# A four-part graph network on one core: its six edge passes rewritten, with sums of parts in PSUM, bf16 scatter, stored one-hots, four gather tiles and a lag of two turns

## What is computed

```
for l in range(3):                                   # message net
    m = concatenate([x[src], x[dst], ew], -1)
    m = relu(m @ edge_W[l] + edge_b[l])
    agg = segment_sum(m, dst, n)
    x = relu(concatenate([x, agg], -1) @ node_W[l] + node_b[l])
...
h0 = relu(x @ W_enc + b_enc)                         # relation net
agg = segment_sum(einsum('nd,rdo->rno', h0, W_rel)[edge_type, src], dst, n)
...
for Wl, b, Wr in ((W1l, b1, W1r), (W2l, b2, W2r)):   # sage net
    h = relu(segment_sum(h[src], dst, n) / deg @ Wl + b + h @ Wr)
```

## Time and profile before

| | |
|---|---|
| median of three runs | 13509.89 us |
| lowest, highest | 13503.28, 13514.92 us |
| span of the profiled execution | 13453.0 us |
| PE, DVE, ACT, POOL busy | 83%, 81%, 39%, 18% |
| TensorE clock granted, mean | 0.949 |
| message passes (first gather to last scatter) | 848, 784, 783 us |
| relation pass | 1220 us |
| sage passes | 566, 566 us |
| from there to the end (attention) | 6314 us |

### The profile page before, as it was taken

How to read it: one execution, slowest core, us unless ns; L and a number is a source line. 1 busy time by engine, 2 the same in 40 slices (tenths; PEclk the granted TensorE clock), 3 DMA queues, 4 the chain that set the end, 5 groups by cost and what they waited for, 6 DMA issues and landing times. The chain is left out here.

```text
span 13453.0 us, 456368 instructions
## 1 busy us (share of the span) xinstructions
PE 11137.4 (83%) x106911; PEld 9882.7 (73%) x106912; DVE 10911.2 (81%) x40164; ACT 5227.5 (39%) x19100; POOL 2409.1 (18%) x7659
## 2 busy tenths in 40 slices
PE   3555399899899599976665879999998789999998
PEld 3444388799798499975553339999997338999998
DVE  6545399688688288876565999999997999999998
ACT  1000022122222022235452338865453337875454
POOL 2777300000000000001110001112221001222222
PEclk9999999899899599999896999999998999999999
DMA  1111177444243011113231554432221554432222
GB/s 54 47 50 47 45 228 236 138 128 128 80 128 115 4 41 41 41 50 88 71 87 51 148 140 115 115 92 73 70 73 47 143 147 113 115 98 73 70 73 61
DMA packets 1206840, 1232.94 MB, mean 92 GB/s; under 512 B 218352, under 2 KB 1042801, under 8 KB 1206107
## 3 DMA queue, kind: packets, MB, share of 16 engines
q1 hardware_dynamic: 1180954, 1228.47, 32.8%
q0 software_dynamic: 25792, 3.35, 0.2%
HBM read 1115.06 MB, written 116.16 MB: 92 GB/s over the span
## 5 line engine op out<-in xcount | busy, mean ns | idle before, releaser
L993 DVE TENSOR_SCALAR hot<-iota_row,place 128x128 f32<-128x128 f16 (+1 forms) x9000 | 1818.8, 269 | 158.5 <-PE acc L1092 135.7
L1711 ACT ACTIVATE msgs<-G,share 128x64 f32<-128x64 f32 x6000 | 1395.6, 315 | 1346.0 <-PE G L1725 1346.0
L985 DVE TENSOR_SCALAR hotT<-idx,iota_col 128x512 bf16<-128x512 f16 x4500 | 1323.8, 352 | 524.4 <-PE G L1138 492.1
L1725 PE MATMUL G<-u_b,hotT 128*128 x12000 | 1592.2, 276 | 50.3 <-DVE hotT L1659 50.3
L1735 PE MATMUL S<-msgs,hot 128*128 128x128 f32 x12000 | 1586.3, 275 | 0.0
L1157 ACT CAST msgs<-G 128x384 bf16<-128x384 f32 x2250 | 1020.4, 480 | 1372.7 <-PE G L1138 1368.1
L1725 PEld LDWEIGHTS G<-u_b,hotT 128*128 128x128 f32 x12000 | 1467.4, 193 | 51.0 <-issue 51.0
L1735 PEld LDWEIGHTS S<-msgs,hot 128*128 128x128 f32 x12000 | 1462.3, 192 | 0.0
L1080 PE MATMUL G<-table_m,hotT 128*128 x9000 | 1309.8, 248 | 93.4 <-issue 69.3
L1110 ACT ACTIVATE msgs<-sums 128x128 f32<-128x128 f32 x2250 | 699.3, 311 | 1762.3 <-DVE sums L1102 1400.5
L1547 ACT ACTIVATE msgs<-G,msgs 128x64 f32<-128x64 f32 x6000 | 1315.5, 333 | 30.5 <-issue 21.0
(11 more groups left out here) (323 smaller groups left out, 19877.9 us busy)
## 6 DMA issues: line engine op xcount, KB each, us to landing
idx<-pos_rows SPq DMA_DIRECT2D x6375, 128.0 KB, 2.9
hotT<-hots_d SPq DMA_DIRECT2D x750, 256.0 KB
hots_d<-hotT SPq DMA_DIRECT2D x375, 256.0 KB, 3.4
key_b<-key_rows SPq DMA_DIRECT2D x62, 416.0 KB
ty_b<-type_rows SPq DMA_DIRECT2D x62, 416.0 KB
rows<-rel_rows SPq DMA_DIRECT2D x1500, 6.0 KB
ew_now<-ew_rows_d SPq DMA_DIRECT2D x1125, 3.0 KB
sorted_d<-recs,place POOLq DMA_INDIRECT x806
```

Source lines behind the costliest of these rows:

```text
L985: op = eng.tensor_scalar(hotT[:, c % deep, n], idx[:, c, r], p.col[:, first:first + 1], None, ALU.is_equal)
L993: op = eng.tensor_scalar(hot[:, c % 2, q], p.row16[:], place[:, c % 2, q:q + 1], None, ALU.is_equal)
L1711: op = eng.activation(msgs[:, c % 2, 2 + j // HEADS, j % HEADS * D:(j % HEADS + 1) * D], G[c % 2][1][:, j * D:(j + 1) * D], ACT.Copy, scal ...
L1725: mm = eng.matmul(G[c % 2][b][:, k * W:(k + 1) * W], hotT[:, c % 2, q * P:(q + 1) * P], table[:, ds(dst_at(at, q, 24 * W), W)], start=True ...
```

## The change

It touches the six passes alone.

- The table's three parts lie one behind the other (`[P, 3, BLK * D]`). In message passes each part is a product of its own of 64 columns, and all seven products of a chunk (three source, three destination, one with nine rows of edge weights) add up in the same 64 columns of `G`, so the reduction on DVE goes. ACT applies the relu from PSUM to an f32 tile `whole`.
- The message is split into three bf16 values for the scatter: the upper halves of `whole`'s words, the upper halves of `left` = whole - upper half, and `low` = left - its upper half, the last two made by DVE. Three bf16 products of 64 columns a chunk replace the f32 one. In the first pass a product of two columns a chunk counts the degrees.
- The first message pass stores its scatter one-hots and source one-hots together; all later passes load the scatter one-hots, the later message passes the source ones too, and these build the destination ones from `idx`. POOL's copies stay in the first pass alone.
- The table `acc` has 64 columns a block (four banks in place of five), and there are four `G` tiles. PE scatters turn t-2 after the gather of turn t. DMAs fetch two turns at a time, and `hots`, `idx` are eight turns deep.
- In the sage passes DVE evicts one half of `G` and ACT the other; in the relation pass ACT does both. A gather product there stays one of 192 columns.

The core of the diff:

```diff
                 def gather(t, c, at):
+                    ready(eng, turned, t + 1)
+                    ready(eng, relud, t + 1)
+                    for q in range(4):
+                        to = G[c % 4][:, q * D:(q + 1) * D]
+                        for side in range(2):
+                            place_of = dst_at(at, q, LAST) if side else src_at(at, LAST)
+                            for part in range(3):
+                                eng.matmul(to, hots[:, c, 1 + side, q * P:(q + 1) * P], s.table3[side][:, part, ds(place_of, D)],
+                                           start=(side == 0 and part == 0), stop=False)
+                        mm = eng.matmul(to, s.ew_now[:, c, q * P:(q + 1) * P], s.we9[:, l], start=False, stop=True)
...
+                def scatter(t, c, was):
+                    ready(eng, made, t + LAG + 1)
+                    for q in range(4):
+                        hot = hots[:, c, 0, q * P:(q + 1) * P]
+                        at = dst_at(was, q, LAST)
+                        to = acc[:, ds(at, D)]
+                        if degrees:
+                            eng.matmul(acc[:, BLK * D:BLK * (D + 2)][:, ds((at >> 5).with_bounds(min_val=0, max_val=LAST >> 5), 2)],
+                                       hot, p.onesb[:], start=False, stop=False, skip_group_check=True)
+                        for of in (top_half(whole[:, c % 4, q:q + 1]), top_half(left[:, c % 4, q:q + 1]), low[:, c % 4, q:q + 1]):
+                            mm = eng.matmul(to, hot, of.rearrange("p k f -> p (k f)"), start=False, stop=False, skip_group_check=True)
...
-                for side in range(2):
-                    mm = eng.matmul(env["G"][h][:, k * 3 * D:(k + 1) * 3 * D],
-                                    env["hotT"][:, c % env["deep"], side, q * P:(q + 1) * P],
-                                    s.table3[side][:, ds(dst_at(at, q, LAST) * 2 if side else src_at(at, 24 * 3 * D), 3 * D)],
-                                    start=(side == 0), stop=False)
...
-                eng.tensor_reduce(sums[:, j], env["G"][h][:, 0:6 * D].rearrange("p (k q f) -> p k f q", q=3, f=D),
-                                  AX.X, ALU.add).then_inc(taken[h].h, 1)
...
+                def remains(t, c):
+                    ready(eng, relud, t + 5)
+                    ready(eng, scattered, t + 1)
+                    eng.tensor_tensor(left[:, c % 4], whole[:, c % 4], top_half(whole[:, c % 4]), ALU.subtract
+                                      ).then_inc(lefted.h, 1)
...
+                def lowest(t, c):
+                    ready(eng, lefted, t + 1)
+                    eng.tensor_tensor(low[:, c % 4], left[:, c % 4], top_half(left[:, c % 4]), ALU.subtract
+                                      ).then_inc(made.h, 1)
...
+                def step(t, c, pair):
+                    remains(t, c)
+                    if not (isinstance(t, int) and t >= Q - 2):
+                        one_hots(t + 2, (c + 2) % 8)
+                    if make:
+                        scatter_hots(t, c)
+                    lowest(t, c)
...
+                    ready(eng, scattered, t - 2)
+                    eng.dma_start(hot[:, c:c + n], s.hots_d[ds(pair, 1), :, 0:n, 0:4 * P].rearrange("o p k e -> (o p) k e")
+                                  ).then_inc(idx_in[c // 2].h, 16)
+                    eng.dma_start(idx[:, c:c + n].rearrange("p k e -> p (k e)"),
+                                  row[ds(t * (4 * P), n * 4 * P)].partition_broadcast(P)).then_inc(idx_in[c // 2].h, 16)
...
+    with eng.Fori(1, QUARTERS // 8) as i:
+        many = load_words(p, eng, 0, i * 8 - lag, lag + 1)
```

More of the change, by code:

```diff
@@ L901, in src_at, with eights @@
     return (words[0] >> 16).with_bounds(min_val=0, max_val=most)
-def edge_pass(p, s, rows, hot_dt, hot_parts, gather, scatter, vector, scalar, finish, extra=None, keep=None, freed=None):
-    ctx = ExitStack()
-    Q, H = QUARTERS, 2
-    NR, NH = len(rows), len(hot_parts)
-    deep = 4 if keep else 2
-    if keep == "load":
-        rows, NR = [], 0
-    ND = NR + (1 if extra else 0) + (1 if keep == "load" else 0)
+def eights(eng, step):
+    for t in range(8):
+        step(t, t, t // 2)
+    with eng.Fori(1, QUARTERS // 8) as i:
+        for c in range(8):
+            step(i * 8 + c, c, i * 4 + c // 2)
+    for t in range(QUARTERS // 8 * 8, QUARTERS):
+        step(t, t % 8, t // 2)
@@ new lines, in first_uses, with ready, quarters_in, top_half @@
+def first_uses(t, c, each):
+    return each * (t // 8) if isinstance(t, int) else (t - c) * (each // 8)
+def ready(eng, sem, count):
+    if not isinstance(count, int) or count > 0:
+        after(eng, sem, count)
+def quarters_in(t):
+    return 1 if isinstance(t, int) and t == QUARTERS - 1 else 2
+def top_half(x):
+    return x.bitcast(BF16).rearrange("p k (f two) -> p k f two", two=2)[:, :, :, 1]
+def clear_sums(eng, p, s, acc):
+    for b in range(4):
+        eng.matmul(acc[:, b * 512:(b + 1) * 512], s.zeros[:, 0:P], s.zeros[:], start=True, stop=True,
+                   skip_group_check=True)
@@ L913, in edge_pass, with gnn_layer @@
+def gnn_layer(p, s, l, degrees):
+    ctx = ExitStack()
+    Q, LAG = QUARTERS, 2
+    make = l == 0
+    rows = [s.pos_rows[0], s.pos_rows[1]] if make else [s.pos_rows[1]]
+    NR = len(rows)
+    ND = NR + 1 + (0 if make else 1)
     with ctx:
-        idx = p.sb("idx", [P, 4, max(NR, 1), 4 * P], FP16, ctx)
-        hotT = p.sb("hotT", [P, deep, NH, 4 * P], BF16, ctx)
-        hot = p.sb("hot", [P, 2, 4, P], hot_dt, ctx)
+        idx = p.sb("idx", [P, 8, NR, 4 * P], FP16, ctx)
+        hots = p.sb("hots", [P, 8, KINDS, 4 * P], BF16, ctx)
@@ new lines, in gnn_layer @@
+        left = p.sb("left", [P, 4, 4, D], FP32, ctx)
+        low = p.sb("low", [P, 4, 4, D], BF16, ctx)
+        acc = p.ps("acc", [P, 4 * 512], ctx)
+        G = [p.ps("G", [P, 512], ctx) for _ in range(4)]
+        idx_in = [p.fresh("positions") for _ in range(4)]
+        stored = [p.fresh("hots_stored") for _ in range(4 if make else 0)]
+        placed, turned, gathered, relud, lefted, made, scattered = (p.fresh(x) for x in (
+            "placed", "gather_hot", "gathered", "relud", "lefted", "made", "scattered"))
@@ L1126, in parts_pass, with step @@
+                def step(t, c, at, was):
+                    if at is not None:
+                        gather(t, c, at)
+                    if was is not None:
+                        scatter(t - LAG, (c - LAG) % 8, was)
+                clear_sums(eng, p, s, acc)
+                for _ in range(4):
+                    eng.nop().then_inc(scattered.h, 1)
+                tensor_turns(p, eng, step, LAG)
 def parts_pass(p, s, row, tables):
     ctx = ExitStack()
+    Q, LAG = QUARTERS, 2
     NT = len(tables)
+    DEEP = 4 if NT == 1 else 2
@@ L1131, in parts_pass @@
+    AHEAD = DEEP // 2
+    ND = 2
     with ctx:
-        msgs = p.sb("msgs", [P, 4, 2, 3, D], BF16, ctx)
-        def gather(eng, c, h, at, env):
-            for k in range(2):
-                q = 2 * h + k
-                for r in range(NT):
-                    mm = eng.matmul(env["G"][h][:, k * 3 * D:(k + 1) * 3 * D],
-                                    env["hotT"][:, c % 2, r, q * P:(q + 1) * P],
-                                    tables[r][:, ds(src_at(at, 24 * 3 * D), 3 * D)], start=(r == 0), stop=(r == NT - 1))
-            return mm
@@ L1773, in message_net @@
         split_stage(p, we[:], [we_parts[:, :, i] for i in range(3)])
-        fetch(p, [(s.we3[i:i + 1], we_parts[:]) for i in range(3)])
+        fetch(p, [(s.we9[i:i + 1], we_parts[:, :, i % EW]) for i in range(EW_ROWS)])
         for l in range(3):
```

422 lines of the change are left out of this document (202 added, 220 removed).

## The result

The changed kernel took 15201.78 us (median of four, 15198.78 to 15207.65) against 13509.05 before: ratio 1.1254, 95% interval 1.1238 to 1.127. It is 1693 us slower; the forecast was 15,075 (+1565), within 14,850 to 15,420.

What follows compares the result with a forecast made beforehand. PE's sequencer was taken to bound four of six changed passes and nearly the first message pass; 624 + 490 + 490 + 24 - 58 - 5 = +1565 us gave 15,075 us, range 14,850 to 15,420 (chance 0.80).

Steps and rivals of the forecast that it cites:

- the 124 of the sum: Price in ns of one added register operation on PE's sequencer: 46 of its own plus a gap of 78.
- The sequencer hardly stood there: Kernel before, message and sage passes: semaphore instructions of 51/51/51 ns read as PE's sequencer hardly waiting.
- The covers: Message passes: work of PE's array, DVE and ACT, said to fit under the sequencer's turn and add no time.
- The prediction's own line on the clock: Message passes at 1.2 GHz: 40 products take 2.3 us, still under the 3.39 us turn; no number changes.
- PE's busy share near half or under: Sign expected in the changed kernel's message passes, which would be longer, if the sequencer bounds them.
- the longer load and the scatter's first operation: Message passes, per turn: 12-word first load in place of 8, 0.03 us; scatter operation working out its block again, 0.04.
- 4 x 0.133: First message pass: four more register operations a turn for the degree columns, each 46 to 65 ns and the gap.
- the ring of PE and DVE: Relation pass: PE and DVE wait on each other, hotT two deep; without four one-hots the array bounds, -58 us.
- hidden sequencer work: Rival for the changed passes: register operations run ahead of the queue, turns fall to the next engine; 12,350 us, chance 0.05.
- half the gap: Rival: register operations in a row cost 85 ns each, message turns 3.00 and 3.40 us; about 14,600 us, chance 0.06.
- The rest: Table layout, fewer larger fetches, no memsets of msgs, one more scatter turn a pass: taken as -5 us.
- The 57 us that the sum put outside the span: Kernel before: difference between the profiled span of 13453.0 us and the median 13509.89, assumed to stay.

Runs made afterwards that it cites:

- the run with one comparison: Kernel before, with a turn's four scatter one-hots made by one 128x512 tensor_tensor comparison in all six passes: 13308.52 us against 13377.27, ratio 0.9948.
- the runs that priced the operation: Changed kernel, three destination products sharing one register operation: 13,906.73 us. Kernel before, each message-pass destination product cut into two of 96 columns: 13,845.08 us.

## Why the prediction was right

**The bound.** Right in what it was used for: in the second message pass operations added to PE's sequencer cost their full time, 127 and 122 ns in two runs for the 124 of the sum. It was too strong as a statement on the kernel before. "The sequencer hardly stood there" rested on semaphore instructions of 51/51/51 ns; but the sage rows above have 51 ns too where the wait was half a microsecond, in the time between the ALU_OP and the semaphore instruction. In the message passes DVE held the sequencer for 0.04 us a turn (the run with one comparison), and in the sage passes, I think, ACT's eviction stood right behind. For an edit that adds, a bound is a bound; for one that removes, the next one has to be known.

**The covers.** Two of them were mis-read, without harm to the sum. The array's 1.17 us a turn was worked out at 29 ns a product, the pace of the relation pass; in the message passes it was 53 ns and 2.1 us. The prediction's own line on the clock had 2.3 us for that pace, still under the turn, and that held. And "PE's busy share near half or under" failed as a sign, 79 to 84%, since overlapping records of 0.24 us fill the time between products that wait for their places. The pitches of 3.4, 1.5 and 3.1, the semaphore rows and DVE's share (46% and 31%) came as signed.

**Message passes 2 and 3.** 3.327 for 3.39. The ten operations at 124 ns make 1.24 us, and the whole turn grew by 1.243: the 0.07 that I had put on top for the longer load and the scatter's first operation didn't show; 0.04 of it may be DVE's hold on the turns of the kernel before (the run with one comparison), which the change took away.

**Message pass 1.** 4.238, over my upper bound of 4.18. The term that was mis-sized is "4 x 0.133": 0.169 each, 0.14 us a turn more (82 ns and a longer gap). And one was missing: the store's effect on TENSOR_LOAD, 0.24 us a turn, 88 us in all. The row was there, since the earlier trace rows has a longest load of 859 ns in just that pass, where the others have about 0.6; I didn't ask why.

**Sage and relation.** 1.531 and 1.534 for 1.534 and 3.113 for 3.09, the ring of PE and DVE as the reason of the second (two runs). The sage transfers fitted: no turn was lost to them. The rivals of hidden sequencer work (12,350 us) and of half the gap (14,600) are out by the runs that priced the operation. The Trainium skill, Advanced Engine Details and Errata, section Sequencer Loop, says that other engine instructions can be read and queued while a control instruction executes; as a rule for products whose place is in a register that is out by the same runs, where each such operation added 0.12 us.

**The rest.** -5 us was the forecast; the medians differ by 1693, the passes by 1646, so it was about +47. The traces show it in three places: the first pass begins some 18 us later in the changed kernel (1612.9 against 1595.2 on one chip), some 17 us lie between the passes, 14 of them behind the third message pass, and the attention part took 6060 to 6075 us from its first to its last load against 6035 to 6062. Its cause was not looked for. The whole was 127 us over the forecast: +120 from the first message pass, -48 from the other two, +8 from relation, -4 from sage and some +51 from here, so it isn't a cancellation of large errors that put it inside the range. The 57 us that the sum put outside the span were no such thing: of the changed kernel's profiled run, 15207.65 us, 15205.8 are span. The first pass began at 1595 to 1688 us in runs of the kernel before and at 1612 to 1740 in runs of the changed one, so the sorting stage varies by more than those 57 us.

## What to carry to other kernels

Count what an engine's sequencer must do for each product, not only the product: where a place comes out of a register, three narrow products in place of one wide one cost three times the place, and here a saving on DVE could not pay for it. PE's busy share was no measure here of what its array needs; the distance of starts was. Before taking work off a bound, find the loop that stands next behind it, by the turns that already run without that work. And where two engines wait for each other over two tiles, two more tiles can bring more than less work does.

## What the runs showed of the hardware

- A TENSOR_LOAD on PE took 0.335 us for 4 words, 0.59 for 8, 0.855 for 12, 1.11 for 16, 1.37 for 20 and 1.62 for 24: 64 ns a word. In the pass that stores 768 KB a pair of turns, every second one of 4 words took some 0.9 to 1.0, and 0.335 again without the store.
- A wait of PE's sequencer on a register's count can stand ahead of the record of the semaphore instruction, whose duration stays at 51 ns.
- Products of 64 columns started 53 ns apart at a granted clock of 0.50 and 29 ns at 1.00, and in the message pass that the sequencer bounds turns took 2.296 and 2.310 us. The second message pass of the changed kernel has 1.00 in its row and starts 53 ns apart, so the distance of starts was the surer sign.
- A register operation that places a product added 0.12 to 0.13 us to a turn that the sequencer bounds, and 0.07 where DVE led.
- A comparison of 128x512 with both operands repeated by a zero stride took 682 ns.
